# A graph network's kernel: last-layer rows gathered while the attention drains, residual through TensorE, sums a pair late

## Chip, cores, metric

The kernel runs on one NeuronCore of a Trainium2 chip. The metric is the device time of one execution in microseconds, the median of several runs. The engines are TensorE (PE, with PEld for its weight loads), VectorE (DVE), ScalarE (ACT), GpSimd (POOL) and SyncE (SP), which issues most of the DMAs. A gather is an indirect DMA that POOL issues.

## What is computed

A graph of 6250 nodes with 128 features and 206250 edges sorted by destination goes through two residual layers. The first is a propagation of five hops, a dense matmul, the residual and a layer norm. The second is an attention over the edges: per edge a key and a value, a score per head, a softmax over the edges of each destination, the weighted sum of values, `Wout`, the residual and a layer norm.

```python
def spmm(h):
    return jax.ops.segment_sum(h[col] * w[:, None], row, num_segments=N)
x = _layernorm(x + (ALPHA * x + coef * sum_of_5_hops) @ weight.T + bias)
...
alpha = jnp.einsum('ehq,qk,ehk->eh', q[dst], Wdot, k)
amax = jax.ops.segment_max(alpha, dst, num_segments=n)
ealpha = jnp.exp(alpha - amax[dst])
denom = jax.ops.segment_sum(ealpha, dst, num_segments=n)
attn = ealpha / denom[dst]
out = jax.ops.segment_sum(attn[..., None] * v, dst, num_segments=n)
x = _layernorm(x + out.reshape(n, DV) @ Wout)
```

## The kernel before

The nodes lie in 49 blocks of 128, the edges in 404 groups of 512 (four tiles of 128). The program is a row of blocks, each with one queue per engine, and a barrier of all engines between two blocks: `find_crowded`, `build_by_lists`, `locate_edges`, `propagate`, `first_layer`, `edge_attention`, `last_layer`. Inside a block the order on each engine is the order in which the code is written, and semaphores (`wait_ge`, `then_inc`) tie the engines to each other. Nothing is scheduled by a tool.

`locate_edges` works out from the sorted destinations where each node's first row lies (`row_first`), and where the rows of each tile's last destination lie (`end_row`, `end_ix`, `end_out`), with many small VectorE instructions.

`first_layer` takes the nodes in 13 quads of four blocks (the last has one). Per quad: `turn` (four transposes), `copy_f`, `multiply`, `measure` (sum, statistics), `root`, `normalise`, a store, `turn_x`, `copy_x`, `queries`, `keep_q`, and four scatters by POOL.

`edge_attention` runs 202 pairs of groups (pair i holds group i and group 202 + i). POOL gathers the eight source tiles of a pair into one of three buffers. The values of a pair come LAG = 7 iterations after its keys, so that the last seven iterations only finish values: `values`, `radial_values` (matmuls into the two-bank ring `ring_ps`), on VectorE `find_spots`, `weigh` and `finish_values`, then `spread_out` (matmuls that sum a tile's edges by destination), a copy to `out_rows` on ScalarE and a store to `sums_table` by SP. I call those seven the drain. Each row of `sums_table` has 128 sums, 8 maxima and 8 denominators. After its last source tile POOL gathers 13 blocks of `end_x`, and waits for the end of the block.

`last_layer` reads `sums_table` back. Every tile's first row (`heads`) is transposed, and four scans of 1616 columns along the tiles join destinations that cross tiles (`top`, `most`, `run_dens`, `sums`). At the same time POOL gathers the first row of every node (`rows`, 49 gathers) and the rows of each tile's end (`ends`, 13). Then 17 units, 13 quads of nodes and 4 of tile ends, go through a pipeline written out step by step. In step u VectorE does `prepare_nodes(u)`, `measure(u-2)`, `invert(u-3)`, TensorE `turn(u)`, `multiply(u-1)`, ScalarE `copy_f(u)`, `root(u-2)`, `normalise(u-3)`. `measure` adds the residual to the product in PSUM (`z`), and releases that PSUM bank with `summed`. There are two banks, `y_ps[u % 2]`, and two `z`. The finished quads of nodes are stored by SP, and after all of these the tile ends are scattered over them by POOL, 13 scatters.

## Times and profile before

| what | us |
|---|---|
| median of 3 runs | 4263.03 (4262.11 to 4264.4) |
| the profiled execution's own time | 4264.13 |
| its span in the trace | 4262.4 |
| `edge_attention` in the trace | 1963.1 to 4122.5 |
| `last_layer` in the trace | 4123.4 to 4262.4 |

The span is read from the trace, and lies 1.7 us below the profiled execution's time and 0.6 us below the median. In a timeline row the first number is the start in us from the span's start, the second the time to the end of the row's last instruction, and x is how many instructions were merged. What stands in brackets is the engine's idle time before, and what ended it.

### The profile page before, as it was taken

To read this page: it belongs to the slowest core of one execution; us is meant where nothing else is said; L and a number is where in the kernel's file an instruction comes from. 1 tells how busy PE (TensorE), PEld (TensorE's weight loads), DVE (VectorE), ACT (ScalarE), POOL (GpSimd) and SP (SyncE) were. 2 spreads that over 40 slices of the span, in tenths; PEclk is the share of its full clock that TensorE was granted. 3 is DMA by queue.
4 is the path that set the end of the run, shared out by engine and by line. 5 is a ranking of instruction groups with operands and counts; after the bars stand their busy time and mean duration, and the time that the engine had idled before them with its cause. 6 is when DMAs were issued, how large, how long until landed. Compare 5 with 4: busy or idle time off the path is not lost. (4 is left out here: it accounts for less than half of the span.)

```text
span 4262.4 us, 74057 instructions
## 1 busy us (share of the span) xinstructions
PE 3865.0 (91%) x26582; PEld 3221.6 (76%) x26582; DVE 2988.8 (70%) x4152; ACT 1979.3 (46%) x2892; POOL 1903.9 (45%) x1994
## 2 busy tenths in 40 slices
PE   4663999999999999974899999999999999999974
PEld 3663999999999999963677777777777777777753
DVE  8996554455444443343788888888888888888865
ACT  5663666566665665531333333333333333333324
POOL 5661000000000000026777777777777777777725
PEclk9886999999999999976999999999999999999986
DMA  6997999999999996514788878777887878777832
GB/s 166 189 189 202 286 291 295 293 295 290 299 296 293 291 294 197 180 61 130 189 218 221 217 216 220 215 215 217 234 216 216 218 216 216 217 219 214 216 122 70
DMA packets 826901, 942.17 MB, mean 221 GB/s; under 512 B 495709, under 2 KB 600297, under 8 KB 826403
## 3 DMA queue, kind: packets, MB, share of 16 engines
q1 hardware_dynamic: 766483, 813.75, 66.0%
q0 software_dynamic: 60048, 123.57, 12.1%
q8 instruction: 221, 3.62, 0.4%
q14 instruction: 149, 1.22, 0.1%
HBM read 646.87 MB, written 289.87 MB: 220 GB/s over the span
## 5 line engine op out<-in xcount | busy, mean ns | idle before, releaser
L2358 POOL DMA_INDIRECT feats_hops<-x_table,src_s x1616 | 1541.1, 954 | 532.2 <-issue 454.2
L1293 PE MATMUL acc<-t_wide,scaled 128*128 128x448 f32 x6860 | 1413.2, 367 | 26.4 <-DVE t_wide L1387 26.4
L1293 PEld LDWEIGHTS acc<-t_wide,scaled 128*128 128x128 f32 x6860 | 1284.9, 188 | 135.0 <-DVE scaled L1405 26.8
L1328 ACT CAST t_wide<-t_ring 128x1568 fp32r<-128x1568 uint8 x490 | 737.5, 1505 | 569.2 <-PE acc L1293 549.2
L1387 DVE CAST t_wide<-t_ring 128x1568 fp32r<-128x1568 uint8 x490 | 478.4, 977 | 737.3 <-PE acc L1293 718.7
L1816 POOL MEMSET l_eps<- 128x1 f32 x1 | 0.1, 103 | 1457.3 <-POOLq L1505 1457.3
L2564 ACT ACTIVATE e_hid_k<-e_turn_ps,e_b 128x512 f32<-128x512 f32 x202 | 139.0, 688 | 596.2 <-PE e_turn_ps L2484 592.7
L2400 PE MATMUL e_turn_ps<-e_weighted,e_spot 128*128 128x128 f32 x3232 | 394.7, 275 | 9.2 <-DVE e_weighted L2628 9.2
L2451 PE MATMUL e_ring_ps<-e_wlin_v,e_x_gv 128*128 128x128 f32 x3232 | 394.0, 275 | 0.4 <-DVE feats_hops L2596 0.4
L2400 PEld LDWEIGHTS e_turn_ps<-e_weighted,e_spot 128*128 128x128 f32 x3232 | 376.8, 192 | 11.2 <-DVE e_weighted L2628 11.2
L2558 ACT COPY e_x_t<-e_turn_ps 128x512 f32<-128x512 f32 x404 | 217.3, 589 | 357.2 <-PE e_turn_ps L2473 352.6
L2534 ACT COPY e_out_rows<-e_turn_ps 128x512 f32<-128x512 f32 x404 | 236.3, 585 | 304.4 <-PE e_turn_ps L2400 299.3
L2451 PEld LDWEIGHTS e_ring_ps<-e_wlin_v,e_x_gv 128*128 128x128 f32 x3232 | 377.1, 192 | 0.7 <-DVE feats_hops L2596 0.7
L2619 DVE TENSOR_TENSOR e_lw<-e_ring_ps,e_w_t 128x1024 f32<-128x1024 f32 x202 | 247.0, 1223 | 141.0 <-PE e_ring_ps L2451 141.0
L2596 DVE TENSOR_TENSOR feats_hops<-e_ring_ps,e_x_t 128x1024 f32<-128x1024 f32 x202 | 246.4, 1220 | 121.1 <-PE e_ring_ps L2501 120.4
L668 PE MATMUL lists_rows_ps<-lists_hot_lo,lists_hot_hi 128*128 128x100 fp8e4 x3200 | 215.5, 235 | 110.2 <-POOL lists_hot_hi L486 89.2
L668 PEld LDWEIGHTS lists_rows_ps<-lists_hot_lo,lists_hot_hi 128*128 128x128 fp8e4 x3200 | 200.5, 110 | 126.5 <-DVE lists_hot_lo L586 78.4
L2609 DVE TENSOR_TENSOR e_spot<-e_iota,e_score_ps 128x1024 f32<-128x1024 f32 x202 | 246.8, 1222 | 23.1 <-PE e_turn_ps L2400 2.8
L2473 PE MATMUL e_turn_ps<-ident,feats_hops 128*128 128x128 f32 x1616 | 212.1, 275 | 56.0 <-DMA feats_hops<-x_table,src_s 56.0
L2640 DVE TENSOR_TENSOR_SCAN feats_hops<-e_same,feats_hops,e_q_ps 128x512 f32<-128x512 f32 x202 | 256.7, 1271 | 0.0
L2501 PE MATMUL e_ring_ps<-e_sh,e_gate_w 128*128 128x512 f32 x808 | 232.1, 399 | 14.9 <-DVE e_prod L2655 14.9
L2600 DVE TENSOR_TENSOR e_x_gv<-e_ring_ps,e_x_t 128x1024 f32<-128x1024 f32 x202 | 245.3, 1214 | 0.0
(298 smaller groups left out, 4894.6 us busy)
## 6 DMA issues: line engine op xcount, KB each, us to landing
t_ring<-adjacency_bytes SPq DMA_DIRECT2D x490, 512.0 KB, 5.7
sums_table<-e_out_rows SPq DMA_DIRECT2D x202, 576.0 KB
q_first<-hop_zeros_q SPq DMA_DIRECT2D x101, 512.0 KB, 5.8
e_sh<-parts_sh SPq DMA_DIRECT2D x404, 128.0 KB
e_ea<-parts_ea SPq DMA_DIRECT2D x404, 128.0 KB
e_q_rows<-q_first SPq DMA_DIRECT2D x202, 256.0 KB, 4.8
e_same<-same_row SPq DMA_DIRECT2D x404, 128.0 KB
adjacency_bytes<-lists_staged SPq DMA_DIRECT2D x196, 256.0 KB, 4.4
```

What stands on the lines that cost most here:

```text
L668: mm = nc.tensor.matmul(rows_ps[t % 2][:, side, col * LO:(col + 1) * LO], his[:, i * P - i % 2 * SLOTS:i * P - i % 2 * SLOTS + P], los[:, ...
L1293: mm = nc.tensor.matmul(acc[c][:, 0:n], U[p][:, b, :], wide[m % WIDE_RING][:, lo:lo + n], start=(b == 0 and p == 0), stop=(b == NB - 1 and ...
L1328: nc.scalar.copy(into, of).then_inc(wide_act, 1)
L1387: nc.vector.tensor_copy(into, of).then_inc(wide_dve, 1)
L2358: nc.gpsimd.indirect_dma_start(x_rows[i % XR][:, g * GT + t, :], None, x1_table, bass.IndirectOffsetOnAxis(ap=src_ix[:, at:at + 1], axis=0 ...
L2400: mm = nc.tensor.matmul(turn_ps[:, h, t * P:(t + 1) * P], spot[j % 2][:, h * GT + t, :], weighted[j % 2][:, h * GT + t, :], start=True, st ...
L2451: mm = nc.tensor.matmul(bank[:, k // GT, at], x_gv[:, j % VR, k // GT, at], wlin_v[:], start=True, stop=True)
L2596: nc.vector.tensor_tensor(x_gk[i % 2][:], ring_ps[(5 * i) % 2][:], x_t[i % 2][:], ALU.mult).then_inc(v_gk, 1)
L2600: nc.vector.tensor_tensor(x_gv[:, i % VR, :, :], ring_ps[(5 * i + 1) % 2][:], x_t[i % 2][:], ALU.mult).then_inc(v_gv, 1)
L2609: nc.vector.tensor_tensor(spot[j % 2][:], iota[:].unsqueeze(1).to_broadcast([P, K, P]), score_ps[:, 2 * P:2 * P + K].unsqueeze(2).to_broad ...
L2619: nc.vector.tensor_tensor(lw[:], ring_ps[(5 * i + 2) % 2][:].rearrange("e g (th c) -> e (g th) c", c=D // H), w_t[n % 2][:, p * K * H:(p + ...
L2640: nc.vector.tensor_tensor_scan(out=q_t[s][:], data0=same[s][:], data1=q_ps[:], initial=q_t[1 - s][:, GE - 1:GE], op0=ALU.mult, op1=ALU.add ...
```

## The change

There are five parts.

1. `locate_edges` also computes, per quad of nodes, how many stores of `sums_table` have to be done before its first rows can be read (`need`), and the flags that say which tile continues the one before (`link_row`, now a DRAM row). The attention no longer loads and compares them.
2. `edge_attention` has POOL gather the 49 first rows after `end_x`, quad by quad (`quad_order`: three quads that need the last stores come last), each quad behind a register load of `need` and a wait on `landed`. SP counts the landings (`see_landed`). At the start of the block SP clears the rows of the last 14 pairs with 14 stores of zeros, and waits for them to land before it goes into its loop.
3. In the drain `spread_out` of a pair is issued one iteration later, and the ring's two banks alternate (`place`), so that the values of the next pair need not wait for the product of this one.
4. `last_layer` gathers the 13 `ends` only. The residual is added by TensorE: each block of `multiply` is an identity matmul of x and the `Wout` matmul, accumulated in the PSUM bank. `z` and `summed` are gone: the statistics and `normalise` read PSUM. The order is changed too: two quads are prepared before the scans, the first unit is measured between them, and the transposes back come at units 4 and 5. The flags are read from `link_row` by the block's first DMA.
5. `first_layer` issues `turn_x` of quad q-2 after `multiply(q)` and `turn(q+2)` (ScalarE's copies follow).

```diff
 first_layer, TensorE:
             for q in range(NQ + 2):
-                if q >= 2:
-                    turn_x(q - 2)
                 if q < NQ:
                     multiply(q)
                 if q + 2 < NQ:
                     turn(q + 2)
                 if q >= 2:
+                    turn_x(q - 2)
                     queries(q - 2)
...
 edge_attention, SP:
+            def see_landed(j):
+                sp.wait_ge(stored[j % 2], 16 * (j // 2 + 1))
+                sp.sem_inc(landed, 1)
             load(0)
             load(1)
+            sp.wait_ge(cleared, 1)
+            for j in range(N - 2 * LAG, N):
+                sp.dma_start(sums_table[j * 2 * GE:(j + 1) * 2 * GE, :].rearrange("(e k) r -> e (k r)", k=K),
+                             out_rows[0][:].rearrange("e k r -> e (k r)")).then_inc(cleared, 16)
+            sp.wait_ge(cleared, 1 + 16 * 2 * LAG)
+            sp.sem_inc(landed, 1)
             for i in ITERATIONS:
                 if on(i - LAG - 1):
                     store(i - LAG - 1)
+                if on(i - LAG - 2):
+                    see_landed(i - LAG - 2)
...
 edge_attention, POOL:
+            for q in quad_order(row_first.shape[1]):
+                stores_needed = pool.value_load(need[0:1, q:q + 1], min_val=2, max_val=N + 1)
+                pool.wait_ge(p_xt, 2 * N)
+                pool.wait_ge(landed, stores_needed)
+                for b in range(4 * q, min(4 * q + 4, row_first.shape[1])):
+                    part, at = row_block(row_parts, b)
+                    nc.gpsimd.indirect_dma_start(
+                        part[:, at, :], None, sums_table,
+                        bass.IndirectOffsetOnAxis(ap=row_first[:, b:b + 1], axis=0)).then_inc(part_got[part_of(q)], 16)
             pool.wait_ge(end_got, 16 * end_x.shape[1])
...
 edge_attention, TensorE:
-                if on(j):
+                if i < N and on(j):
                     spread_out(j, i)
+                if i > N and on(j - 1):
+                    spread_out(j - 1, i)
...
 last_layer, SP:
             clear_spent(sp, spent)
+            sp.dma_start(link[:, 1:TILES + 1], link_row[:, 0:TILES].to_broadcast([P, TILES])).then_inc(link_in, 16)
...
 last_layer, TensorE:
             def multiply(u):
+                _, _, x, _, b0, n = unit(u)
+                if u >= 2:
+                    pe.wait_ge(normalised, u - 1)
+                if u == 0:
+                    pe.wait_ge(x_in, 16)
                 pe.wait_ge(f_copied, u + 1)
-                if u >= 2:
-                    pe.wait_ge(summed, u - 1)
-                for j in range(UNITS[u][1]):
-                    mm = nc.tensor.matmul(y_ps[u % 2][:, j * D:(j + 1) * D], f_t[u % 2][:, j, :], w[:], start=True, stop=True)
+                for j in range(n):
+                    nc.tensor.matmul(y_ps[u % 2][:, j * D:(j + 1) * D], ident[:], x[:, b0 + j, :], start=True, stop=False)
+                    mm = nc.tensor.matmul(y_ps[u % 2][:, j * D:(j + 1) * D], f_t[u % 2][:, j, :], w[:], start=False, stop=True)
                 mm.then_inc(multiplied, 1)
...
 last_layer, ScalarE (normalise) and VectorE (measure):
-                    last = nc.scalar.activation(into[:, b + j, :], z[u % 2][:, j, :], ACT.Identity,
+                    last = nc.scalar.activation(into[:, b + j, :], y_ps[u % 2][:, j * D:(j + 1) * D], ACT.Identity,
...
-                nc.vector.tensor_tensor(z[s][:, 0:n, :], y_ps[s][:, 0:n * D].rearrange("p (j d) -> p j d", d=D),
-                                        res[:, b:b + n, :], ALU.add).then_inc(summed, 1)
-                dve.wait_ge(summed, u + 1)
                 for j in range(n):
-                    last = nc.vector.bn_stats(stats[s][:, j, :], z[s][:, j, :])
+                    last = nc.vector.bn_stats(stats[s][:, j, :], y_ps[s][:, j * D:(j + 1) * D])
```

How the order moves, first on POOL, at the passage from the attention to the last layer. Before:

```order
L2358 DMA feats_hops<-x_table,src_s 128x128 x1616
L2362 DMA x_res<-x_table,end_ix 128x128 x13
L2196 UNCONDITIONAL_BRANCH
L2832 UNCONDITIONAL_BRANCH
L2834 MEMSET o_ones 8x128
L2835 MEMSET o_sums 128x49
L2836 MEMSET o_run_dens 8x49
L2837 MEMSET o_most 8x49
L2840 AFFINE_SELECT o_spread<-o_ones 8x128
L2843 AFFINE_SELECT o_spread<-o_spread 8x128
L2845 MEMSET o_eps 128x1
L2850 DMA o_rows<-sums_table,row_first 128x144 x49
```

After, at the same place (the three rows from L2427 on come 13 times, and the branches after the last of them):

```order
L2419 DMA feats_hops<-x1_table,src_s 128x128 x1616
L2423 DMA x_res<-x1_table,end_ix 128x128 x13
L2427 TENSOR_LOAD need
L2427 ISA x2
L2432 DMA x_res<-sums_table,row_first 128x144 x4
```

The 49 gathers of first rows moved from behind the barrier to ahead of it, each quad with a register load and its waits.

TensorE in the last layer, from the matmuls that spread the exponentials over the features (`o_spread`) on. Before:

```order
L2911 MATMUL o_sum_ps<-o_top,o_spread 128x404 x4
L2880 MATMUL o_f_ps<-ident,o_rows 128x128 x8
L2888 MATMUL o_y_ps<-o_w,feats_hops 128x128 x4
L2924 MATMUL o_head_ps<-ident,o_most 128x8 x13
L2924 MATMUL o_head_ps<-ident,o_run_dens 128x8 x13
```

After:

```order
L2998 MATMUL o_sum_ps<-o_top,o_spread 128x404 x2
L2998 MATMUL o_head_ps<-o_top,o_spread 128x404 x2
L2970 MATMUL o_y_ps<-o_x_nodes,ident 128x128
L2971 MATMUL o_y_ps<-o_w,feats_hops 128x128
L2970 MATMUL o_y_ps<-o_x_nodes,ident 128x128
L2971 MATMUL o_y_ps<-o_w,feats_hops 128x128
```

The transposes of the first two units went ahead of the spreading, and each block of a unit now has two matmuls where it had one.

TensorE in the first layer, from the third multiplication on. Before:

```order
L1866 MATMUL l_x_ps<-ident,x_res 128x128 x4
L1858 MATMUL l_y_ps<-l_w,l_f_t 128x128 x4
L1850 MATMUL l_f_ps<-ident,feats_hops 128x128 x4
L1876 MATMUL l_q_ps<-l_wqd,l_x_t 128x64 x4
L1866 MATMUL l_x_ps<-ident,x_res 128x128 x4
```

After:

```order
L1861 MATMUL l_y_ps<-l_w,l_f_t 128x128 x4
L1853 MATMUL l_f_ps<-ident,feats_hops 128x128 x4
L1869 MATMUL l_x_ps<-ident,x_res 128x128 x4
L1879 MATMUL l_q_ps<-l_wqd,l_x_t 128x64 x4
L1861 MATMUL l_y_ps<-l_w,l_f_t 128x128 x4
```

The transposes of x moved from ahead of the multiplication to directly ahead of the queries that need them.

## Rows read from the trace of the kernel before

**Rows 1.** The page: span, and lines of the chain that ended last.

```profile
span 4262.4 us, 74057 instructions
...
POOL o_rows L2850 1%; POOL out L2858 0%; POOL o_ends L2850 0%; DMA o_ends<-sums_table,end_row 0%; PE o_f_ps L2880 0%; PE o_y_ps L2888 0%; ACT o_x_nodes L2965 0%; ACT x_res L2965 0%; DVE o_ends L3037 0%; DVE o_ends L3032 0%; ACT L2959 0%; DVE feats_hops L3032 0%; DVE o_stats L3049 0%; DVE feats_hops L3045 0%; POOL o_sums L2835 0%
```

**Rows 2.** Busy time by stretch; after the engines the granted clock (1.00: 2.4 GHz), DMA.

```profile
1871.00:1899.00 28.00, 21.67 (x99) 20.92 (x100) 16.30 (x77) 7.71 (x18) 12.64 (x13) 0.50 0.21 63
...
2060.00:4050.00 1990.00, 1974.94 (x14904) 1514.10 (x14902) 1730.70 (x1924) 777.45 (x1538) 1478.11 (x1551) 1.00 0.80 218
4157.00:4245.00 88.00, 42.37 (x221) 38.16 (x221) 58.85 (x230) 44.72 (x105) 50.35 (x51) 0.64 0.30 78
```

**Rows 3.** Timeline of TensorE in the first layer: two steps' `turn_x`, and queries.

```profile
1891.86 1.12 PE L1866 MATMUL l_x_ps<-ident,x_res 128*128 128x128 f32 x4 [1.30 <-DVE x_res L1968]
...
1898.43 0.90 PE L1866 MATMUL l_x_ps<-ident,x_res 128*128 128x128 f32 x3 [1.30 <-DVE x_res L1968]
...
1941.41 1.97 PE L1876 MATMUL l_q_ps<-l_wqd,l_x_t 128*128 128x64 f32 x8 [0.68 <-ACT l_x_t L1911]
```

**Rows 4.** Timeline, from the end of `locate_edges` into the next block.

```profile
399.86 1.84 DVE L2179 SCALAR_TENSOR_TENSOR src_s<-s_src_low,s_src_high 128x1616 int32<-128x1616 int32 x1
402.82 0.15 POOL L1367 MEMSET hop_zeros_q<- 128x64 f32 x1 [32.34 <-POOLq L1998]
```

**Rows 5.** Attention's start: timeline; then DMA issues of 4123 to 4145.

```profile
1971.02 1.11 SPq L2311 DMA_DIRECT2D e_same<-same_row  x2
...
2001.24 0.73 PE L2484 MATMUL e_turn_ps<-e_ea,e_stack 128*128 128x512 f32 x2
...
o_x_nodes<-x_table SPq DMA_DIRECT2D x1, 3136.0 KB, 14.7
```

**Rows 6.** Timelines of POOL and TensorE around the start of the attention's drain.

```profile
4052.10 0.95 POOL L2362 DMA_INDIRECT x_res<-x_table,end_ix  x1 [0.30 <-issue]
...
4057.00 1.04 PE L2473 MATMUL e_turn_ps<-ident,feats_hops 128*128 128x128 f32 x8
...
4084.53 2.05 PE L2400 MATMUL e_turn_ps<-e_weighted,e_spot 128*128 128x128 f32 x16 [1.54 <-DVE e_weighted L2628]
```

**Rows 7.** Timeline of the last layer's first part, up to the last scan.

```profile
4123.41 1.00 DVE L3067 TENSOR_SCALAR o_apart<-x_res 8x1617 f32<-8x1617 f32 x1 [4.53 <-PEq L2196]
...
4144.45 1.55 ACT L2946 ACTIVATE o_top<-o_drop 8x1616 f32<-8x1616 f32 x1 [2.07 <-DVE o_drop L3080]
...
4146.03 1.83 DVE L3084 TENSOR_TENSOR o_dens<-o_dens,o_top 8x1616 f32<-8x1616 f32 x1 [0.40 <-ACT o_top L2946]
...
4146.10 3.03 PE L2911 MATMUL o_sum_ps<-o_top,o_spread 8*128 8x404 f32 x4 [4.62 <-ACT o_top L2946]
...
4151.34 1.02 DVE L3091 TENSOR_TENSOR o_sums<-o_sum_ps,o_sums 128x404 f32<-128x404 f32 x2
...
4156.74 3.52 DVE L3094 TENSOR_TENSOR_SCAN o_sums<-x_res,o_sums 128x1616 f32<-128x1616 f32 x1
```

**Rows 8.** Timeline of single units of the last layer.

```profile
4171.03 0.69 DVE L3045 TENSOR_TENSOR feats_hops<-o_y_ps,o_x_nodes 128x512 f32<-128x512 f32 x1 [0.75 <-ACT o_x_nodes L2965]
...
4173.33 1.65 ACT L2965 ACTIVATE o_x_nodes<-feats_hops,o_off,o_rs 128x128 f32<-128x128 f32 x4
...
4175.08 0.69 DVE L3045 TENSOR_TENSOR feats_hops<-o_y_ps,o_x_nodes 128x512 f32<-128x512 f32 x1 [0.57 <-ACT o_x_nodes L2965]
...
4189.56 0.35 DVE L3003 RECIPROCAL o_inverse<-o_rows 128x32 f32<-128x32 f32 x1 [2.62 <-DMA o_rows<-sums_table,row_first]
...
4190.79 0.68 DVE L3045 TENSOR_TENSOR feats_hops<-o_y_ps,o_x_nodes 128x512 f32<-128x512 f32 x1
...
4191.83 1.92 PE L2888 MATMUL o_y_ps<-o_w,feats_hops 128*128 128x128 f32 x8
```

**Rows 9.** Timeline of POOL: first and last of the 13 scatters at the end.

```profile
4238.31 1.00 POOL L2858 DMA_INDIRECT out<-x_res,end_out  x1 [22.73 <-ACT x_res L2965]
...
4253.61 0.96 POOL L2858 DMA_INDIRECT out<-x_res,end_out  x1 [0.30 <-issue]
```

More of the change, by code:

```diff
@@ L2181, in _, with quad_order, part_of, row_block @@
             dve.wait_ge(src_set, 3)
+PART_COUNT = 7
+def quad_order(blocks):
+    quads = -(-blocks // 4)
+    late = (quads // 2 - 1, quads // 2, quads - 1)
+    return [q for q in range(quads) if q not in late] + list(late)
+def part_of(q):
+    return min(quad_order(49).index(q) // 2, PART_COUNT - 1)
+def row_block(row_parts, b):
+    return (row_parts[0], b) if b < row_parts[0].shape[1] else (row_parts[1], b - row_parts[0].shape[1])
 def edge_attention(nc, att, feats, a, whole_sem, spent, parts, x1_table, src_ix, q_first, same_row, neg_table, keep_table, sums_table, ident,
-                   fpos, end_x, end_ix, link, link_later, G):
+                   fpos, end_x, end_ix, row_first, need, row_parts, G):
     N = G // 2
@@ L2392, in spread_out @@
                 pe.wait_ge(v_weighted, j + 1)
[L2393 to L2394 removed]
+                for turned in (i - 3, i - 2):
+                    if not on(i + 1) and chain_at(turned) is not None:
+                        pe.wait_ge(a_wt, 3 * chain_at(turned) + 3)
                 for h in range(2):
```

249 lines of the change are left out of this document (141 added, 108 removed).

## Prediction

> **What bounds the kernel now.** The page comes first: the span is 4262.4 us, and the chain that ended last names the gathers of the last layer, its units and its scatters [rows 1]. Then the busy time by stretch: TensorE is busy 1974.94 of 1990 us in the attention, at 2.4 GHz, so nothing there moves unless TensorE's own work or its start does; in the units of the last layer no engine is near full, and TensorE has 42.37 of 88 us at a mean granted clock of 0.64, a mixture of 1.2 and 2.4 GHz [rows 2]. A stretch in which nobody is busy is bound by a cycle of waits, so the timelines of the two layers' steps were read next. In the last layer VectorE waits up to 2.62 us for gathers; where it doesn't, one unit follows the next after 4175.08 - 4171.03 = 4.05 us, and what ends its idle time is ScalarE's `normalise` [rows 8]. The last layer takes 4262.4 - 4123.4 = 139.0 us [rows 1, 7].
>
> **First layer: 6 us less.** A step takes 1898.43 - 1891.86 = 6.57 us, of which TensorE waits 1.30 us for `x_res` ahead of `turn_x` [rows 3]. With `turn_x` behind `multiply` and `turn` that wait goes. What is late next is ScalarE's `copy_x`, which used to lie under the multiplication: the wait ahead of the queries is 0.68 us where nothing covers it [rows 3]. So 1.30 - 0.68 = 0.6 us less per quad, 0.4 us if the rows' overlaps are counted against it; 12 quads give 5 to 7 us, and a start without the first wait about 1 us. The clock in the dense part is 0.50 [rows 2]; a change of level moves this by some us either way. I take -6, with 0 to -11.
>
> **Flags and `need`: 1.5 us more.** VectorE ends the block (1.84 us for 1616 columns) [rows 4]. The change puts about eight instructions on a few columns into its row, at a tenth of that each, and transposes and one small DMA beside it. +1.5, with +0.5 to +4.
>
> **Clearing at the attention's start: 1 us more.** SP has issued its first two loads by 1971.02 + 1.11 = 1972.1 [rows 5]. Then come 14 stores of 128 x 1152 x 4 B = 0.59 MB, 8.3 MB in all. The nearest row is the 3.2 MB load that took 14.7 us [rows 5], so 14.7 x 8.3 / 3.2 = 38 us at most, and perhaps 28 us if the engines do better with a deep queue; the third pair's load is issued only behind them, at 2000 to 2010, and its hidden matmul, at 2001.24 now [rows 5], comes 7 to 15 us late. Behind it wait TensorE and VectorE, but not POOL: it has three buffers and goes on. These first iterations have no values to finish, so that TensorE can catch up before the pairs become full. I take +1, from 0 to +15 (none of it caught up).
>
> **The drain: nothing.** TensorE waits 1.54 us per pair for the product [rows 6]. With the sums a pair late this goes, some 1.5 x 6 = 9 us. But the block ends with the last of its engines, and now that is POOL. It may touch the lent buffers only when the last source tiles are turned, at 4057.00 + 1.04 = 4058.0; a gather takes 0.95 + 0.30 = 1.25 us [rows 6], 49 of them 61.5 us. To this come 13 register loads. The trace has none alone; a barrier, a register load and a branch lie between 401.70 and 402.82 [rows 4], so a load is at most 1.1 us, and at least 0; I take 0.5, since most of the 1.1 must be the barrier: 6.5 us (0 to 14). The Trainium skill, DMA: Bandwidth & Descriptors (Latency and other measured facts), gives a floor of about 600 ns for a `tensor_load`; by that page it would be 7.8 us, an estimate, and no row here shows one by itself. With 1 us of barrier the last layer starts at 4058.0 + 61.5 + 6.5 + 1 = 4127, and at 4127 - 6 + 1.5 + 1 = 4123.5 with the shifts from above (4115 to 4145). It starts now at 4123.4. The 49 gathers are gone from the last layer, but its start is where it was.
>
> **The last layer, up to the fourth unit.** Count from its start. Today the exponential ends at 4144.45 + 1.55 = 4146.0, 22.6 us in [rows 7]. The flags (128 x 6.5 KB = 0.83 MB) now lie ahead of the heads in SP's queue: 14.7 x 0.83 / 3.2 = 3.8 us at the rate of [rows 5], taken as 3; the two quads that VectorE prepares meanwhile hide in the wait. So 25.6. The spreading takes 3.0 us [rows 7], and then the first `multiply`. It has eight matmuls where it had four: 16 instructions for eight 128x128 matmuls take 2.05 us at 2.4 GHz [rows 6], and 8 take 1.92 us at 1.2 GHz [rows 8], so 3.7 us for 16. The first unit's statistics start at 25.6 + 0.1 + 3.0 + 3.7 = 32.4. VectorE then needs: statistics 1.35 (the sum of 0.69 is gone), the product 1.83 and a scan of 3.5, to 39.1; 1.2 for `prepare_nodes` (4190.79 - 4189.56), statistics 1.35, reciprocals 0.35, to 42.0; four products, 0.51 to 0.58 each, and a scan of 3.52, to 47.8; `prepare_nodes`, to 49.0 [rows 7, 8]. Unit 3 starts a cycle later, at 55.3.
>
> **The cycle of the units, the step that decides.** Two PSUM banks serve the units. Before, the bank was given back by the sum into `z`, so that `multiply` ran beside the rest, and the 4.05 us are sum, statistics, reciprocals and `normalise` (1.65 us) [rows 8]. Now ScalarE's `normalise` reads the bank, and `multiply(u+1)` waits for `normalise(u-1)`. In VectorE's order `invert(u-1)` stands behind `measure(u)`, and `measure(u)` behind `multiply(u)`. So every unit is one chain: multiply, measure, invert, normalise, and then the next multiply. The cycle is 4.05 - 0.7 (the sum) + the eight matmuls: 4.05 - 0.7 + 2.05 = 5.4 us at 2.4 GHz, and 4.05 - 0.7 + 3.7 = 7.05 us at 1.2 GHz; there `copy_f` reaches ScalarE so late that `root` can wait for it, 7.4 us. The clock is not in any row of the changed loop. TensorE would be busy some 4.8 of 7.1 us, somewhat more than the 42.37 of 88 with which it has 0.64 now [rows 2]. At 0.64 a third of the time is at 2.4 GHz: the cycle is 6.6 us, which I take.
>
> **To the end.** From unit 3 to unit 15 are 12 cycles. Extra: ScalarE copies the scans' results at unit 5 (2.4), the ends' shares (4); less: the quad of one block (-4). Together +2.4, say 3. From unit 15's statistics: 7.0 us until it is normalised (its own rest, and the one-block unit 16 ahead), 0.8 to POOL, four more scatters of 1.27, (4253.61 - 4238.31) / 12, and from the last scatter to the end 4262.4 - 4253.61 = 8.8 [rows 9]. That is 21.7. The last layer: 55.3 + 3 + 21.7 + 12 x 6.6 = 159.2 us, against 139.0.
>
> **Sum.** 4123.5 + 159.2 = 4282.7 us of span; the median lies 0.6 us above the span of the trace before, so 4283.3, 20 us or 0.5% slower.
>
> **Rivals.**
>
> *The cycle runs at 2.4 GHz.* Then it is 5.4 us, and the time 14.4 us less: 4269. For it speaks that `multiply` becomes a dense block twice as long; against it the first layer, where TensorE is busy 21.67 of 28 us at 0.50 [rows 2]. The Trainium skill, TensorE: Matmul & The Clock Gate (What's actually happening), says that the default is the throttled state and sustained activity releases it; by that page the change would pay part of its cost back, and this rival is what it would give; the first layer's row doesn't agree with it. 13%, between same and slower.
>
> *The units were bound by gathers, and the hand-over of the bank costs nothing.* This ends faster. If `multiply` still found its bank free, the 12 cycles would be 4.05 us or less, and the last layer 80 + 49 = 129 us: 4253. It decides from a cycle of about 4.5 us down. For it: up to 2.62 us of waits for gathers per unit today [rows 8], all of which go. Against it: two banks, and a wait on `normalised` of the unit two before in the code. With a first layer 5 us better it is the only way I see to a clear gain. 9%.
>
> *The clearing is not caught up.* 8.3 MB in the queue beside the first gathers, and the pairs' loads behind: the attention starts up to 15 us later, and since TensorE is full afterwards it stays so: 4298. Point of decision: whether the turns of the eighth pair come later than now. 13%.
>
> *POOL is held in the drain* (register loads of 1 us, or a store that lands late): 7 to 10 us more, 4292, within the forecast's own range. 10%.
>
> **Chances.** The forecast with its clock between the levels (4274 to 4292) 55%, full clock 13%, free bank 9%, clearing 13%, POOL held 10%. This measurement can tell about 0.2%, 8.5 us, from no change. Faster than 4254.5 is the free bank without losses elsewhere, 8%. Between 4254.5 and 4271.5 are the full clock and the better half of the first layer's range, 16%. Slower: 76%. The range takes in the full clock at the low end with some of the first layer's bound, and the clearing at the high end: 4262 to 4299.
>
> **What would show it right or wrong.** In the profile of the changed kernel: (1) TensorE's `multiply` rows in the last layer wait for ScalarE's `normalise`, and one `bn_stats` group starts 5.4 to 7.4 us after the last; 4 us would make the prediction wrong. (2) The last layer's first instruction stands at 4115 to 4130, with POOL's gathers ending just before; if it stood at 4100 the drain would have counted. (3) The exponential ends 25 to 26 us after that. (4) No `turn_x` in the first layer waits 1.3 us, and the attention's first pair begins 3 to 8 us earlier. (5) The attention's third hidden matmul is late, the eighth pair's turn is not. (6) The granted clock in the units is 0.5 to 0.8.

## The result, and the profile after

| | median, us | ratio to before | 95% interval |
|---|---|---|---|
| before | 4263.03 | | |
| changed | 4274.74 | 1.0027 | 1.0017 to 1.0036 |

The changed kernel is 11.7 us slower. The span of its profiled execution is 4273.4 us, against 4262.4 before: +11.0. Read at the borders of the stages, this is the sum of five terms:

| stage | before | after | difference | predicted |
|---|---|---|---|---|
| up to `propagate` | 402.82 | 404.48 | +1.7 | +1.5 |
| from there to the attention's first gather | 1561.1 | 1540.3 | -20.9 | -6 |
| from there to the last turns of source rows | 2093.1 | 2095.7 | +2.6 | +1 |
| from there to the last layer's start | 66.4 | 72.4 | +6.0 | +3.6 |
| last layer | 139.0 | 160.6 | +21.6 | +20.2 |

The page of the changed kernel, its span and the chain that ended last. Where the chain of before began with GpSimd's gathers [rows 1], it now has the last layer's `multiply` (L2970, L2971) at its head:

```profile
span 4273.4 us, 74573 instructions
...
PE o_y_ps L2970 1%; PE o_y_ps L2971 0%; ACT o_x_nodes L3048 0%; DMA o_heads<-sums_table 0%; DVE o_stats L3128 0%; POOL out L2937 0%; PE o_f_ps L2959 0%; ACT o_sd L3042 0%; DVE o_sums L3188 0%; ACT feats_hops L3037 0%; DVE o_run_dens L3180 0
```

Busy time by stretch in the same kernel, columns as in [rows 2]; the first stretch is the dense part of the first layer, the second the units of the last:

```profile
1871.00:1899.00 28.00, 22.05 (x171) 19.00 (x172) 26.61 (x127) 12.84 (x30) 18.45 (x19) 1.00 0.33 96
...
4157.00:4245.00 88.00, 52.92 (x266) 48.50 (x267) 40.01 (x165) 31.80 (x81) 0.00 (x0) 0.67 0.13 36
```

In the first layer TensorE is busy as long as before (22.05 of 28 us, 21.67 before), but does 171 instead of 99 pieces of work in it; its granted clock is 1.00 and not 0.50. In the units TensorE's busy time rose from 42.37 to 52.92 us, and that of VectorE, ScalarE and GpSimd fell, in part because fewer units fall into these 88 us.

TensorE in the first layer, two steps of the changed kernel:

```profile
1875.60 0.60 PE L1869 MATMUL l_x_ps<-ident,x_res 128*128 128x128 f32 x4
1876.92 1.10 PE L1879 MATMUL l_q_ps<-l_wqd,l_x_t 128*128 128x64 f32 x8 [0.73 <-ACT l_x_t L1913]
1877.87 1.11 PE L1861 MATMUL l_y_ps<-l_w,l_f_t 128*128 128x128 f32 x8
1878.81 0.60 PE L1853 MATMUL l_f_ps<-ident,feats_hops 128*128 128x128 f32 x4
1879.60 0.66 PE L1869 MATMUL l_x_ps<-ident,x_res 128*128 128x128 f32 x4 [0.18 <-DVE x_res L1970]
```

The wait of 1.30 us ahead of `turn_x` [rows 3] is gone, the wait of about 0.7 us ahead of the queries has come, as worked out. But the step is 1879.60 - 1875.60 = 4.0 us, where it was 6.57.

GpSimd at the end of the attention and the start of the last layer, timeline of the changed kernel:

```profile
4041.68 0.95 POOL L2432 DMA_INDIRECT x_res<-sums_table,row_first  x1 [5.24 <-PE e_turn_ps L2547]
...
4100.11 0.95 POOL L2432 DMA_INDIRECT x_res<-sums_table,row_first  x1 [3.41 <-issue]
...
4105.13 0.95 POOL L2432 DMA_INDIRECT feats_hops<-sums_table,row_first  x1 [0.31 <-issue]
4112.78 0.19 POOL L2916 MEMSET o_ones<- 8x128 f32 x1 [6.70 <-POOLq L2246]
```

The gathers start when the last source rows are turned and keep a pace of 1.26 us. One wait of 3.41 us stands ahead of the first late quad. After the last gather nothing is in the timeline for 6.70 us. What ends them is shown by the instructions of the block's last line, a DRAIN on each engine's queue (name, count, duration in ns, start; the two latest):

```profile
L2246 SPq DRAIN  x1: 7/7/7, 4098.6 to 4098.6; - x1
L2246 POOLq DRAIN  x1: 10022/10022/10022, 4102.5 to 4102.5; - x1
```

All other engines are done by 4098.6. GpSimd's queue reaches its DRAIN at 4102.5, ahead of its own engine, and stays in it for 10.0 us, to 4112.5.

Two units of the last layer after, timeline of all three engines (some rows of a row of eight matmuls left out):

```profile
4186.89 0.89 DVE L3128 BATCH_NORM_STATS2 o_stats<-o_y_ps 128x6 f32<-128x128 f32 x4 [6.12 <-PE o_y_ps L2971]
...
4188.49 1.51 ACT L3048 ACTIVATE o_x_nodes<-o_y_ps,o_off,o_rs 128x128 f32<-128x128 f32 x4
...
4190.05 0.80 PE L2970 MATMUL o_y_ps<-o_x_nodes,ident 128*128 128x128 f32 x2 [2.76 <-ACT o_x_nodes L3048]
...
4190.64 0.64 PE L2971 MATMUL o_y_ps<-o_w,feats_hops 128*128 128x128 f32 x2
...
4193.20 0.41 PE L2971 MATMUL o_y_ps<-o_w,feats_hops 128*128 128x128 f32 x2
...
4193.64 0.89 DVE L3128 BATCH_NORM_STATS2 o_stats<-o_y_ps 128x6 f32<-128x128 f32 x4 [3.97 <-PE o_y_ps L2971]
```

This is a closed chain of waits: statistics wait for the product (3.97 us), the next product for `normalise` (2.76 us). It goes round in 6.75 to 6.82 us; the corresponding rows of before are 4.05 us apart where no gather is waited for [rows 8].

### The profile page after: what moved, and what is told of

It reads as the page before. It is cut to its first block and busy times, and to the rows that moved or that the text cites. A ratio compares the mean times of both kernels' runs of the same rounds, so it can differ in the third digit from the quotient of the medians.

```text
span 4273.4 us, 74573 instructions
## 1 busy us (share of the span) xinstructions
PE 3875.2 (91%) x26709; PEld 3233.1 (76%) x26709; DVE 2977.5 (70%) x4143; ACT 1977.1 (46%) x2892; POOL 1900.2 (44%) x1994
## 5 line engine op out<-in xcount | busy, mean ns | idle before, releaser
L2575 PE MATMUL e_ring_ps<-e_sh,e_gate_w 128*128 128x512 f32 x808 | 233.0, 400 | 16.8 <-DVE e_prod L2736 16.8
```

## Experiments

Two theories. **A**: the loss is the units' closed chain, that is, the bank that is held until `normalise`; it hides a gain of some 20 us in the first layer. **B**: it is the extra matmuls' own time, or the edges around the stage (the rearranged start, late gathers, clearing, register loads). The medians of before in the four groups of runs were 4264.3 (e1 to e4), 4264.0 (e5 to e8), 4264.1 (e9 to e11) and 4263.4 us (e12).

| kernel | median, us | ratio to before | 95% interval |
|---|---|---|---|
| e1, before with part 5 alone | 4245.72 | 0.9960 | 0.9946 to 0.9973 |
| e2, residual on VectorE | 4241.94 | 0.9945 | 0.9929 to 0.9960 |
| e3, matmul, bank given back early | 4244.93 | 0.9953 | 0.9938 to 0.9968 |
| e4, no matmul, bank held | 4265.88 | 1.0002 | 0.9993 to 1.0012 |
| e5, sums not late | 4283.70 | 1.0046 | 1.0030 to 1.0061 |
| e6, late quads in the last layer | 4262.91 | 0.9999 | 0.9990 to 1.0009 |
| e7, cleared twice as much | 4286.91 | 1.0065 | 1.0044 to 1.0086 |
| e8, four banks | 4247.40 | 0.9963 | 0.9950 to 0.9975 |
| e9, register loads four times | 4273.78 | 1.0024 | 1.0014 to 1.0034 |
| e10, e2 with four late quads | 4229.19 | 0.9922 | 0.9905 to 0.9939 |
| e11, e10 with four banks from unit 6 | 4223.25 | 0.9907 | 0.9891 to 0.9924 |
| e12, before with TensorE's half of part 5 | 4246.36 | 0.9960 | 0.9946 to 0.9975 |

### e1 and e12: the first layer's order alone

The edit to the kernel before; e12 has this alone, in e1 ScalarE's copies follow as in the change:

```diff
             for q in range(NQ + 2):
-                if q >= 2:
-                    turn_x(q - 2)
                 if q < NQ:
                     multiply(q)
                 if q + 2 < NQ:
                     turn(q + 2)
                 if q >= 2:
+                    turn_x(q - 2)
                     queries(q - 2)
```

> The kernel before with part 5 alone: in the first layer turn_x stands behind multiply and turn, and ScalarE's copies follow. Theory A, the order of this one layer gives the whole gain seen at the attention's start in the changed kernel: the attention's first gather moves from 1963.9 to about 1943 us, TensorE's granted clock in 1871 to 1899 rises above 0.50, and the time is about 4242 us. Theory B, my prediction's term (6 us, one hidden wait per quad, the clock left as it is): first gather at 1958, time 4257; then the other 14 us of the changed kernel come from its other parts. Besides: the changed kernel loses 2.3 us of its lead between the 8th and the last pair of the attention. If this kernel loses them too, it is not the counting of the landings.

The time fell by 18.6 us. The first gather of the attention is at 1947.2, 16.8 us earlier. Busy time by stretch of this kernel, and one of the first scatters in GpSimd's timeline:

```profile
1871.00:1899.00 28.00, 21.13 (x164) 18.10 (x163) 26.68 (x128) 12.83 (x29) 16.43 (x17) 1.00 0.32 96
```

```profile
1879.62 0.98 POOL L1840 DMA_INDIRECT q_first<-l_q_all,q_place  x1 [0.30 <-issue]
```

Theory A holds: the order of this one layer gives 17 to 19 us, and the clock is 1.00. The layer's block, from GpSimd's first instruction in it to the attention's first gather, takes 103.6 us before, 85.8 in the changed kernel, 86.2 in e1 and 84.5 in e12. So 17.8 of the 20.9 us of the stage table lie here. The other 3.1 lie in `propagate`, which takes 1457.6 us before, 1457.9 and 1460.1 in e1 and e12, and 1452.6 to 1456.5 in the changed kernel and the ten made from it. Why is not shown.

The layer ends with GpSimd. In e1 its scatters follow each other from 1879.62 on with 0.30 us between them, 1.27 us each, so the layer is now bound by them, and 2.6 us less per step of TensorE do not come through in full. In the kernel before GpSimd waits 0.7 to 1.9 us for ScalarE's copy of the queries ahead of nine quads, 11.2 us beyond the usual 0.30, and once, near the end, for a store of them. These waits are what went. The second kind, and TensorE's first two pauses of over 2 us in its steps, in timelines of the kernel before:

```profile
1955.18 0.98 POOL L1837 DMA_INDIRECT l_mid_q<-q_table,l_mid_ix  x1 [6.28 <-DMA q_table<-l_q_all]
```

```profile
1872.13 1.12 PE L1866 MATMUL l_x_ps<-ident,x_res 128*128 128x128 f32 x4 [3.75 <-DVE x_res L1968]
...
1905.01 1.11 PE L1866 MATMUL l_x_ps<-ident,x_res 128*128 128x128 f32 x4 [2.38 <-DVE x_res L1968]
```

The step of 6.57 us before was itself a closed chain: `turn_x` stands ahead of `multiply`, VectorE's sum waits for `multiply` (2.9 us), and only behind this sum, in VectorE's order, comes the `normalise` for which the next `turn_x` waits. From 1901 on the rows behind `multiply` ran at 2.4 GHz in some steps (queries 1.00 us in place of 1.81), and the step stayed at 1905.01 - 1898.43 = 6.58 us, with a pause of 2.38 us in place of 1.30. Part 5 takes `turn_x` out of this chain.

> The kernel before with TensorE's half of part 5 alone: turn_x behind multiply and turn, ScalarE's copies in the order of before. Theory A, the clock rises because the pause ahead of turn_x, which stood between the queries and the next multiplication in every step, is gone: granted clock in 1871 to 1899 near 1.00, the same gain as with both halves, 4245 to 4248 us. Theory B, ScalarE's order is needed: copy_x first holds copy_f back until turn_x is done, TensorE waits ahead of the next multiply instead, the clock stays near 0.50 and the step near 6 us: 4256 to 4266 us.

TensorE's half is enough: 17.0 us less than before, first gather at 1947.3. Busy time by stretch, and TensorE's timeline with a step at each level:

```profile
1871.00:1899.00 28.00, 21.65 (x158) 19.47 (x158) 25.72 (x127) 12.35 (x29) 15.61 (x16) 0.92 0.30 88
```

```profile
1883.53 0.66 PE L1866 MATMUL l_x_ps<-ident,x_res 128*128 128x128 f32 x4 [0.54 <-DVE x_res L1967]
1884.86 1.10 PE L1876 MATMUL l_q_ps<-l_wqd,l_x_t 128*128 128x64 f32 x8 [0.68 <-ACT l_x_t L1910]
1885.81 1.97 PE L1858 MATMUL l_y_ps<-l_w,l_f_t 128*128 128x128 f32 x8
...
1891.05 1.11 PE L1858 MATMUL l_y_ps<-l_w,l_f_t 128*128 128x128 f32 x8
```

Here the clock fell once, for one step, behind pauses of 0.54 and 0.68 us, and rose again. In the kernel before it fell behind the one pause of 3.75 us ahead of the first `turn_x`, stayed at 0.50 until 1901 with a pause of 1.30 us per step, and then rose and fell with the steps. In the changed kernel, e1 and e12 the pause at the first `turn_x` is 1.39, 1.35 and 1.59 us, and the clock stays at 1.00 behind it. The new order shortens both pauses, the first one and that of each step; no run separates them.

### e2, e3, e4: the matmul and the bank apart

The three kernels restore `z`. In e2 the residual goes back to VectorE and the bank is given back by the sum. e3 keeps the identity matmuls, and VectorE copies the bank to `z` and gives it back. e4 has no identity matmuls, but `multiply` waits for `normalise` all the same.

```diff
 multiply, e2:
-                    pe.wait_ge(normalised, u - 1)
+                    pe.wait_ge(summed, u - 1)
...
-                    nc.tensor.matmul(y_ps[u % 2][:, j * D:(j + 1) * D], ident[:], x[:, b0 + j, :], start=True, stop=False)
-                    mm = nc.tensor.matmul(y_ps[u % 2][:, j * D:(j + 1) * D], f_t[u % 2][:, j, :], w[:], start=False, stop=True)
+                    mm = nc.tensor.matmul(y_ps[u % 2][:, j * D:(j + 1) * D], f_t[u % 2][:, j, :], w[:], start=True, stop=True)
 measure, e2 and e4:
+                nc.vector.tensor_tensor(z[s][:, 0:n, :], y_ps[s][:, 0:n * D].rearrange("p (j d) -> p j d", d=D),
+                                        x[:, b:b + n, :], ALU.add).then_inc(summed, 1)
 measure, e3:
+                nc.vector.tensor_copy(z[s][:, 0:n, :], y_ps[s][:, 0:n * D].rearrange("p (j d) -> p j d", d=D)).then_inc(summed, 1)
 normalise, all three:
-                    last = nc.scalar.activation(into[:, b + j, :], y_ps[u % 2][:, j * D:(j + 1) * D], ACT.Identity,
+                    last = nc.scalar.activation(into[:, b + j, :], z[u % 2][:, j, :], ACT.Identity,
```

> The changed kernel, but in the last layer the residual is added by VectorE again: one matmul per block, the sum into z (0.69 us) gives the bank back, statistics and normalise read z. Theory A, the units' cycle through the bank is the loss: a unit follows the next after about 4.05 us in place of 6.80, 12 to 14 units long, so the last layer takes 160.6 - 33 to 38 = 123 to 128 us and the time is about 4238 to 4243 us. Theory B, the loss of the last layer lies in its rearranged start and in waits for GpSimd: the cycle falls, but less than 10 us of the time go, about 4267.

> The changed kernel with the identity matmul kept, but VectorE copies each unit's bank into z (0.69 us) and gives the bank back then; statistics and normalise read z. Theory A, what costs is that the bank is held until normalise: TensorE's work goes beside the rest again and a unit takes 4.1 to 5.5 us (the upper end if TensorE's own row of four transposes and eight matmuls at 1.2 GHz becomes the bound), time 4244 to 4257. Theory B, what costs is the extra matmuls themselves: the cycle stays at 6.8 less nothing, plus the copy: 6.8 to 7.5, time 4275 to 4283.

> The changed kernel without the identity matmuls (VectorE adds the residual into z), but multiply still waits for the normalise of the unit two before, as if the bank were held. Theory A, the hand-over: the four matmuls (1.92 us for 8 instructions at 1.2 GHz) stand in the chain of every unit, so the cycle is 4.05 + 1.0 to 1.9 = 5.1 to 6.0 us, the time 4253 to 4264. Theory B, the extra matmuls: the cycle is about 4.1 and the time about 4240, the same as with the bank given back early.

| | identity matmuls | bank held until | cycle, us | last layer, us |
|---|---|---|---|---|
| changed | yes | normalise | 6.80 | 160.6 |
| e3 | yes | copy | 4.05 | 131.7 |
| e4 | no | normalise | 6.12 | 153.3 |
| e2 | no | sum | 4.05 | 130.8 |

With the bank given back the identity matmuls cost nothing in the cycle, 4.05 us with them and without (the whole layer is 0.9 us longer with them, and the medians lie 3.0 us apart). With the bank held even half of the matmuls cost 2.07 us per unit. The three kernels come out as theory A has it. TensorE in e3, then, in e4, two of VectorE's sums into `z` and between them a `multiply` (timelines):

```profile
4187.84 0.66 PE L2960 MATMUL o_f_ps<-ident,x_res 128*128 128x128 f32 x4 [1.61 <-DVE x_res L3090]
4188.33 0.39 PE L2971 MATMUL o_y_ps<-o_x_nodes,ident 128*128 128x128 f32 x2
4188.55 0.39 PE L2972 MATMUL o_y_ps<-o_w,feats_hops 128*128 128x128 f32 x2
...
4191.89 0.66 PE L2960 MATMUL o_f_ps<-ident,x_res 128*128 128x128 f32 x4 [1.61 <-DVE x_res L3090]
```

```profile
4200.55 0.69 DVE L3127 TENSOR_TENSOR feats_hops<-o_y_ps,o_x_nodes 128x512 f32<-128x512 f32 x1 [2.64 <-PE o_y_ps L2971]
...
4204.55 1.51 PE L2971 MATMUL o_y_ps<-o_w,feats_hops 128*128 128x128 f32 x8 [3.19 <-ACT o_x_nodes L3048]
...
4206.10 0.69 DVE L3127 TENSOR_TENSOR feats_hops<-o_y_ps,o_x_nodes 128x512 f32<-128x512 f32 x1 [2.07 <-PE o_y_ps L2971]
```

In e4 the rows of four matmuls ahead of this one took 2.08 us each, at 1.2 GHz throughout, and the sum waited 2.64 us for them; that is the cycle of 6.12 us. The one shown ran in part at 2.4 GHz, and its unit took 5.5 us.

A row of two matmul instructions takes 0.39 us in e3 and 0.63 to 0.64 for most of a unit in the changed kernel. In e3 TensorE stands still 1.61 us of 4.05 and runs at 2.4 GHz, in the changed kernel 2.76 of 6.8, in e4 3.19 of 6.12. So the closed chain costs twice: it puts the matmuls in line, and it makes the pauses after which they run mostly at 1.2 GHz in these two kernels.

### e5: the drain without its new order

`spread_out(j, i)` is issued in its own iteration again, `place` returns `5 * i + n`, and ScalarE's order follows:

```diff
...
-                if i < N and on(j):
+                if on(j):
                     spread_out(j, i)
-                if i > N and on(j - 1):
-                    spread_out(j - 1, i)
...
```

> The changed kernel with part 3 undone: in the drain spread_out of a pair is issued in its own iteration again and the ring's banks follow the old pattern. Theory A, the last stores' landing holds GpSimd's last quads, so the drain is on the path after all: in the kernel before, TensorE's last sums end 62.2 us after the start of the last turns, in the changed one 53.8; the stall ahead of GpSimd's last five gathers grows from 3.4 to about 12 us, the last layer starts 8 us later and the time is about 4283 us. Theory B, my prediction's term: the drain hides behind GpSimd's gathers, and the time stays at 4275.

9.0 us slower than the changed kernel, as theory A has it. GpSimd's timeline in this kernel at the first late quad and at the start of the last layer:

```profile
4105.11 0.95 POOL L2432 DMA_INDIRECT x_res<-sums_table,row_first  x1 [11.29 <-issue]
...
4110.15 0.95 POOL L2432 DMA_INDIRECT feats_hops<-sums_table,row_first  x1 [0.30 <-issue]
4117.80 0.20 POOL L2911 MEMSET o_ones<- 8x128 f32 x1 [6.70 <-POOLq L2246]
```

The stall of 3.41 us has grown to 11.29: the drain is on the path through the landing of its last stores.

### e6: the three late quads gathered in the last layer

```diff
-            for q in quad_order(row_first.shape[1]):
+            for q in quad_order(row_first.shape[1])[:-3]:
...
 last_layer, POOL, behind the 13 ends:
+            for q in quad_order(NB)[-3:]:
+                for b in range(4 * q, min(4 * q + 4, NB)):
+                    part, at = row_block(row_parts, b)
+                    nc.gpsimd.indirect_dma_start(
+                        part[:, at, :], None, sums_table,
+                        bass.IndirectOffsetOnAxis(ap=row_first[:, b:b + 1], axis=0)).then_inc(got[part_of(q)], 16)
```

> The changed kernel, but the nine blocks of the three quads that need the last stores are gathered in the last layer, behind the tile ends; 40 stay in the attention. Theory A, what starts the last layer late is GpSimd's tail: a stall of 3.4 us for a landing, five gathers, and a DRAIN that ends 6.4 us behind the last gather. Without them GpSimd's last gather ends near 4093 and its DRAIN near 4099, the last store is seen landed at 4098.3, and the last layer starts at about 4100 in place of 4112.8: time 4262. The nine gathers (11.3 us) end long before unit 10 needs them. Theory B, the start waits for something else at the block's end, or the gathers take away from the last layer what they give back: at most 3 us less, 4272.

4262.91 us, 11.8 less than the changed kernel. From the last turns to the last layer's start it is 60.6 us in place of 72.4, and the last layer takes 162.0. But the DRAIN was not 6.4 us behind the last gather, as expected. GpSimd's last gather here and its DRAIN (timeline; instructions of the last line):

```profile
4092.88 0.95 POOL L2432 DMA_INDIRECT feats_hops<-sums_table,row_first  x1 [0.30 <-issue]
```

```profile
L2246 POOLq DRAIN  x1: 23900/23900/23900, 4078.9 to 4078.9; - x1
L2246 SPq DRAIN  x1: 7/7/7, 4100.3 to 4100.3; - x1
```

It ends at 4102.8, 9.0 us behind the last gather, and is still what everybody waits for, 2.5 us longer than SP. So a fourth quad was moved in e10 and e11; there GpSimd's DRAIN ends 8.7 us behind its last gather, 2.9 us before SP reaches its own.

### e7: clearing twice as much

```diff
-            for j in range(N - 2 * LAG, N):
+            for j in range(N - 4 * LAG, N):
...
-            sp.wait_ge(cleared, 1 + 16 * 2 * LAG)
+            sp.wait_ge(cleared, 1 + 16 * 4 * LAG)
```

> The changed kernel with 28 stores of zeros at the attention's start in place of 14 (16.6 MB in place of 8.3). Theory A, the clearing is caught up before the pairs become full: the first turns may come some us later, the eighth pair's turn not more than 1 us, time 4275 to 4277. Theory B, the rival of the prediction, clearing delays the pairs for good: what 14 stores cost is then added once more, and since the stores take some 20 us, the time is 5 to 20 us longer.

12.2 us slower than the changed kernel: theory B for the doubled size. Its five runs lie further apart than those of any other kernel here, from 4284.0 to 4302.6. SP's queue at the block's start (the issue of the stores, and the first instruction behind the wait for their landing), and TensorE's longest waits in 1955 to 2060 (who waits for whom: us in total, times, longest), in this kernel:

```profile
1951.98 37.62 SPq L2391 DMA_DIRECT2D sums_table<-e_out_rows  x28
2002.35 0.56 SPq L2374 DMA_DIRECT2D e_neg<-neg_table  x1
```

```profile
PE e_turn_ps L2547 <- DMA feats_hops<-x_table,src_s: 51.9, 4, 40.1
PE e_turn_ps L2558 <- DMA e_ea<-parts_ea: 23.1, 1, 23.1
```

The same two views of the changed kernel:

```profile
1952.97 16.48 SPq L2391 DMA_DIRECT2D sums_table<-e_out_rows  x14
1981.74 0.56 SPq L2374 DMA_DIRECT2D e_neg<-neg_table  x1
```

```profile
PE e_turn_ps L2547 <- DMA feats_hops<-x_table,src_s: 61.8, 7, 41.4
PE e_turn_ps L2558 <- DMA e_ea<-parts_ea: 2.7, 1, 2.7
```

Fourteen stores hold SP for 28.8 us, 28 for 50.4. With 28.8 us the third pair's loads (`e_ea` is one of them) come late in the shadow of the first gathers, for which TensorE waits anyway: it waits 2.7 us for `e_ea`, and less for the gathers right behind it. With 50 us it waits 23.1 for `e_ea`, more than the gathers leave. From the first gather to the last turns it is 2091.4 to 2093.2 us in the three kernels without clearing (before, e1, e12), 2093.3 to 2096.3 in the ten with 14 stores, 2107.1 with 28. So the clearing and the counting of the landings together cost 2 us in the mean. The traces divide them. The eighth pair is turned 82.2 us after the first gather in the mean of the three without clearing, 82.4 in that of the ten, 94.6 with 28 stores; from there to the last turns it is 2010.3, 2012.0 and 2012.4 us. So the 14 stores cost about 0.2 us, and the rest comes in the pairs behind them, where SP counts the landings; no run has the counting alone.

### e8: four banks

```diff
+        def y_bank(u):
+            return y_ps[u % 2] if u < 6 else (y_ps + head_ps)[u % 4]
...
-                if u >= 2:
-                    pe.wait_ge(normalised, u - 1)
+                if u in (6, 7):
+                    pe.wait_ge(rows_kept, 2)
+                elif u >= 2:
+                    pe.wait_ge(normalised, u - 1 if u < 6 else u - 3)
...
```

`multiply`, the statistics and `normalise` take their bank from `y_bank`.

> The changed kernel, residual by TensorE and statistics and normalise reading PSUM, but from unit 6 on the units use four banks in turn (the two of head_ps are free by then), so multiply waits for the normalise of the unit four before. Theory A, the closed chain is the loss and any way out of it will do: the cycle falls from 6.80 to between 4.1 us (VectorE and ScalarE as in the kernels with z) and 5.5 us (TensorE's transposes and eight matmuls at 1.2 GHz): ten units, 13 to 27 us less, 4248 to 4262. Theory B, another edge of the chain holds it (invert behind measure, the statistics' buffers): no less than 6.3 us, time 4270 or more.

27.3 us less than the changed kernel, somewhat beyond the expected range, because the cycle is 3.20 us and not 4.1. VectorE and TensorE of this kernel:

```profile
4187.79 0.89 DVE L3133 BATCH_NORM_STATS2 o_stats<-o_head_ps 128x6 f32<-128x128 f32 x4 [0.42 <-ACT o_x_nodes L3053]
...
4190.63 0.66 PE L2962 MATMUL o_f_ps<-ident,feats_hops 128*128 128x128 f32 x4 [0.75 <-DVE feats_hops L3094]
4191.00 0.89 DVE L3133 BATCH_NORM_STATS2 o_stats<-o_head_ps 128x6 f32<-128x128 f32 x4 [0.43 <-ACT o_x_nodes L3053]
```

TensorE pauses 0.75 us and keeps 2.4 GHz. The cycle is 0.85 us shorter than any with `z`. The rows account for it: the sum or copy of 0.69 us is off VectorE (0.73 from its start to that of the statistics), and `normalise` takes 1.50 us from the bank and 1.65 from `z`. So moving the residual to TensorE is a gain, if the banks are there.

### e9: register loads four times

```diff
-                stores_needed = pool.value_load(need[0:1, q:q + 1], min_val=2, max_val=N + 1)
+                for _ in range(4):
+                    stores_needed = pool.value_load(need[0:1, q:q + 1], min_val=2, max_val=N + 1)
```

> The changed kernel with each of the 13 register loads of need issued four times in a row. In the trace of the changed kernel a load is 0.29 us and its register operations 0.15 us on GpSimd's queue. Theory A, the queue is some 3.6 us ahead of the engine, so the loads lie beside the making of the descriptors: the gathers of the drain keep their pace of 1.26 us, only the loads behind the one stall show (up to 3 us), time 4275 to 4278. Theory B, the term of my prediction, where every load adds to the row of gathers: 3 x 13 x 0.44 = 17 us more, time 4292.

4273.78 us, the same as the changed kernel. The loads in GpSimd's queue (count, shortest, median and longest ns, first and last start), and in its timeline the one stall of the drain:

```profile
L2428 POOLq TENSOR_LOAD <-need x52: 282/288/867, 4017.3 to 4099.2; - x52
```

```profile
4096.43 0.95 POOL L2433 DMA_INDIRECT x_res<-sums_table,row_first  x1 [3.87 <-issue]
```

The 39 additional loads can be seen and cost at most the 0.46 us by which the stall is longer. The Trainium skill, DMA: Bandwidth & Descriptors (Latency and other measured facts), gives a floor of about 600 ns for one; here it is 0.29 us in the median, and beside the gathers none of it is felt.

### e10 and e11: a version that beats both

e10 is e2 with four quads (13 blocks) gathered in the last layer. e11 is e10 with `z` for the units below 6 only, and the identity matmuls and four banks of e8 from unit 6 on.

> The changed kernel with the residual on VectorE and four quads (13 blocks) gathered in the last layer, both as tried apart before (there 4241.9 and, with three quads, 4262.9 us). Theory A, the two are independent: the last layer starts when SP has seen the last store land, some 2.6 us earlier than with three quads, and the time is 4241.9 - 11.8 - 2.6 = 4227.5. Theory B, one gives back a part of the other (the 26 gathers of the last layer beside VectorE's units, or GpSimd's DRAIN that is as long with fewer gathers): 4231 to 4240.

> As the kernel before in this list (four quads gathered in the last layer), with the residual on VectorE for the first six units, while the scans hold the other banks, and from unit 6 on by TensorE with four banks in turn. Theory A: units 0 to 5 as with VectorE (stats of unit 6 some 70 us after the layer's start), then a cycle of 3.2 us in place of 4.05 for about eight units: 6 to 7 us less than the kernel before, 4221. Theory B, TensorE's clock is lower there than with four banks in the kernel without z, so that the cycle is 4 us or more: no gain over the kernel before, 4228.

4229.19 and 4223.25 us. Both gains add up in e10 (expected 4227.5), and the four banks give another 6 us (expected 4221): in e11 the cycle is 3.20 us from unit 7 to unit 10 (3.3 to 3.7 in the two ahead), and the last layer takes 125.4 us, from 4096.7. e11 is 0.93% faster than the kernel before (interval 0.76 to 1.09%).

## Why the prediction came out as it did

It forecast 4283, slower, with a range of 4262 to 4299; the time is 4274.74. The mechanism on which it rested, the closed chain of the units, held. The span is 9.3 us below the forecast one: `propagate` and the first layer 14.9 less than forecast, and 5.6 more from the rest (attention +1.6, its end +2.4, last layer +1.4, flags +0.2). That the time still lies in the range is owed to the room left for the clock of the units, not to any for the first layer: this part is luck. Of the six signs four came out as written; the attention began 19.2 us earlier, not 3 to 8, and with it the last layer stood at 4112.8, 2 us ahead of its 4115 to 4130.

- **The cycle of the units.** Right in its mechanism (shown by e2, e3, e4 and e8) and nearly so in its size: 6.6 predicted, 6.80 measured. The 6.6 came from a mean clock of 0.64 between 5.4 and 7.05 us. The rows show how that goes wrong: the mean clock after is 0.67, but most of a `multiply` runs at 1.2 GHz (0.63 us per pair) and only its last rows at 2.4. A stretch's mean clock counts the pauses too. With the measured 3.56 us for the row of matmuls (4190.05 to 4193.61) the same sum gives 4.05 - 0.7 + 3.56 = 6.9.
- **The last layer's other steps.** From its start to the exponential's end 25.0 us (25.6 predicted), to the first statistics 33.8 (32.4), to unit 3's 56.9 (55.3), from there to unit 15's 85.3 (82.2), from those to the end 18.4 (21.7). The last term was too large because 8.8 us were taken from the last scatter's start to the end [rows 9]; after, the last scatter starts at 4268.54 and the end is 4.9 us later. Sum 160.6, against 159.2.
- **First layer: the mis-sized term.** -6 predicted, -20.9 in the trace (-17.8 in the layer's own block), -17 to -19 for the order alone (e1, e12). The step that failed is the clause "a change of level moves this by some us either way": the waits were worked out rightly, but with rows at 1.2 GHz kept as they were. The clock went to 1.00 and a matmul row from 1.91 to 1.11 us, and the layer gained about three times what the waits were worth. The range (0 to -11) had no place for it, though [rows 2] showed the clock at 0.50. GpSimd's waits, which the gain is made of, were not in the working at all. That the same order with the clock at 0.50 would have given the 6 us was not run.
- **The drain: nothing.** Wrong as a term (e5: 9.0 us), and not to be seen in the total, since against the kernel before it is offset by the tail that the change adds. The prediction let GpSimd run through its 49 gathers without a stop. But the late quads wait for the last stores to land, so TensorE's drain stays on the path through them.
- **The last layer's start.** From the end of the last turns 71.4 us, 69 predicted, out of three wrong pieces: register loads 6.5 predicted, none felt (e9); a stall of 3.4 us for the last stores' landing, not in the sum (the rival that POOL is held priced it at 7 to 10); and at the block's end 1 predicted and 6.7 measured, for GpSimd's DRAIN. In the kernel before this DRAIN is there too, but lay in 70 us of idle time, and no row of the timeline shows it.
- **Flags and `need`.** +1.5 predicted, +1.7 measured (in the ten kernels made from the changed one the next block starts 0.6 to 1.8 us later than before; in e1 and e12, without the flags, 0.3 later and 0.2 earlier).
- **Clearing.** +1 predicted; about 0.2 measured up to the eighth pair and 1.7 in the pairs behind it. "Perhaps 28 us" for the 14 stores was 28.8. The rival of a clearing that is not caught up was wrong for this size and right for twice this size (e7): it begins somewhere between 29 and 50 us of a blocked SP.
- **Free bank, the rival on the other side.** Its first half was true: without the gathers' waits the last layer is 130.8 us in e2, 8.2 less than before. Its second, that the hand-over costs nothing, was false.
- **Full clock.** The rival that held that the cycle would run at 2.4 GHz was wrong for the changed loop and right for the open one. The Trainium skill, TensorE: Matmul & The Clock Gate (What's actually happening), says that the throttled state is the default and activity releases it; the rows of the units are in line with it: e3 and e8, with pauses of 1.61 and 0.75 us per unit, are at 2.4 GHz, the changed kernel with 2.76 us is mostly at 1.2. The first layer's busy 22 of 28 us at either clock shows that the busy share alone does not tell which.

## What to carry to other kernels

Work moved to an engine that has time is free only while the buffer that it writes is given back as early as before: when a later reader takes over from an early copy, count who waits for the bank, or have more banks first. Where a stage runs at half of TensorE's clock, cost an edit at both levels, because removing a pause can be worth far more through the clock than through the pause. Look also for the engine that ends the stage: here it was GpSimd, and its waits set what a faster step was worth. And before gathers are put at the end of a block, look at what they wait for and at GpSimd's DRAIN behind them: the last gathers are better left to the next block.

## What the hardware showed that was not expected

- GpSimd's DRAIN at the attention's end lasts until 6.4 to 6.5 us after the last gather's row where a stall came shortly before (changed kernel, e5, e9) and 8.5 to 9.0 us where none did (before, e6, e10, e11). Nothing in the timeline but the DRAIN's own duration shows it.
- Register loads on GpSimd's queue (0.29 us each) cost nothing beside gathers, even 52 of them.
- TensorE with 22 us of work in 28 ran at 1.2 GHz in one order and at 2.4 GHz in another. TensorE's order alone does it (e12). It shortens one pause of 3.75 us at the layer's start and one of 1.30 us in each step, and which of them counts is open; so is why pauses of 1.39 and 1.22 us ahead of the changed kernel's first queries are borne at 2.4 GHz, and in e12 one step with 0.54 and 0.68 us is not.
- Two gathers of tile ends in the changed kernel's last layer took 4.2 and 3.2 us in place of 0.95 while VectorE ran scans of 1616 columns; two gathers of first rows in the kernel before took 4.2 and 3.2 us beside the same scans. No run isolated it.
